# Attention over eight heads: turns of one key tile, with weighing on halves of the rows, in place of double steps

## The reference

```python
def _L0_conv_ref(x, Wq, Wk, Wv, Wsc, gamma):
    q = jnp.einsum('bchw,oc->bohw', x, Wq).reshape(b, HEADS, dq, n)
    k = jnp.einsum('bchw,oc->bohw', x, Wk).reshape(b, HEADS, dq, n)
    v = jnp.einsum('bchw,oc->bohw', x, Wv).reshape(b, HEADS, dv, n)
    attn = jax.nn.softmax(jnp.einsum('bhdn,bhdm->bhnm', q, k), axis=-1)
    out = jnp.einsum('bhnm,bhdm->bnhd', attn, v)
    out = out.reshape(b, w, h, HEADS * dv).transpose(0, 3, 1, 2)
    sc = jnp.einsum('bchw,oc->bohw', x, Wsc)
    return gamma * out + sc

x = x + _L0_conv_ref(_gn(x), Wq, Wk, Wv, Wsc, gamma)
```

## Time and profile before

| | |
|---|---|
| median of 3 runs | 3122.99 us (3122.82 to 3123.27) |
| profiled execution: span | 3120.7 us, 119616 instructions |
| busy: TensorE / weight loads | 3078.5 us (99%) / 2183.3 us (70%) |
| busy: VectorE / ScalarE / POOL | 2284.6 (73%) / 2244.3 (72%) / 2787.6 us (89%) |
| DMA | 110.78 MB, 35 GB/s in the mean |

### The profile page before, as it was taken

How to read it: one execution, slowest core, us unless ns; L and a number is a source line. 1 busy time by engine, 2 the same in 40 slices (tenths; PEclk the granted TensorE clock), 3 DMA queues, 4 the chain that set the end, 5 groups by cost and what they waited for, 6 DMA issues and landing times.

```text
span 3120.7 us, 119616 instructions
## 1 busy us (share of the span) xinstructions
PE 3078.5 (99%) x52307; PEld 2183.3 (70%) x52307; DVE 2284.6 (73%) x3624; ACT 2244.3 (72%) x4020; POOL 2787.6 (89%) x2039
## 2 busy tenths in 40 slices
PE   6999999999999999999999999999999999999998
PEld 4677777767777677777777777777776777767766
DVE  7777777777787777777777777777777777777774
ACT  5676787777676777777667677778776767667676
POOL 1788999999898899999889899999988989889899
PEclk9999999999999999999999999999999999999999
DMA  3111110110112011110112111111101010101011
GB/s 130 31 40 39 30 47 23 45 34 23 36 40 59 20 38 41 27 53 25 24 33 57 40 29 41 38 31 46 23 25 24 22 27 20 29 20 28 21 29 30
DMA packets 168968, 110.78 MB, mean 35 GB/s; under 512 B 120320, under 2 KB 166400, under 8 KB 168448
## 3 DMA queue, kind: packets, MB, share of 16 engines
q1 hardware_dynamic: 168448, 103.13, 12.6%
HBM read 56.10 MB, written 18.87 MB: 24 GB/s over the span
## 4 chain that ended last, share of the span: by engine, by line
PE 91%; POOL 5%; ACT 0%; issue 0%; DVE 0%; ACTq 0%; DVEq 0%
PE SL L441 25%; PE PJ L380 19%; PE MX L413 11%; PE OB L465 10%; PE OB L462 9%; PE OB L464 9%; PE PJ L377 6%; POOL PLO L954 5%; PE SL L436 1%; ACT PE L558 0%; POOL half L950 0%; ACT L676 0%; DVE mx L753 0%; DVE PLO L923 0%; PE SL L389 0%
## 5 line engine op out<-in xcount | busy, mean ns | idle before, releaser
L954 POOL TENSOR_TENSOR PLO<-PE 128x768 f16<-128x768 f32 x1727 | 2551.0, 1500 | 266.8 <-ACT PE L558 255.5
L558 ACT ACTIVATE PE<-SL 128x768 f32<-128x768 f32 x1728 | 1307.3, 809 | 27.6 <-PE SL L441 27.5
L462 PE MATMUL OB<-V,PE 128*128 128x65 f16 x10368 | 1048.5, 193 | 6.8 <-POOL PLO L954 5.7
L464 PE MATMUL OB<-V,PE 128*128 128x64 f16 x10368 | 1048.5, 193 | 0.0
L465 PE MATMUL OB<-V,PLO 128*128 128x65 f16 x10368 | 1048.2, 196 | 0.0
L462 PEld LDWEIGHTS OB<-V,PE 128*128 128x128 bf16 x10368 | 965.1, 99 | 58.2 <-POOL PLO L954 11.7
L441 PE MATMUL SL<-QK 64*128 64x384 f16 x10368 | 1000.8, 323 | 0.1
L464 PEld LDWEIGHTS OB<-V,PE 128*128 128x128 bf16 x10368 | 962.5, 97 | 42.9
L566 ACT ACTIVATE MXC<-MX 128x384 f32<-128x384 f32 x864 | 423.3, 490 | 752.2 <-PE MX L413 752.2
L465 PEld LDWEIGHTS OB<-V,PLO 128*128 128x128 f16 x10368 | 963.4, 98 | 0.0
L753 DVE TENSOR_REDUCE mx<-MX 128x2 f32<-128x768 f32 x864 | 828.4, 959 | 84.4 <-PE MX L413 38.0
(11 more groups left out here) (105 smaller groups left out, 1237.9 us busy)
## 6 DMA issues: line engine op xcount, KB each, us to landing
gx<-x SPq DMA_DIRECT2D x36, 768.0 KB, 4.7
xr<-x SPq DMA_DIRECT2D x96, 192.0 KB, 2.4
out<-xr SPq DMA_DIRECT2D x96, 192.0 KB, 1.9
X<-x SPq DMA_DIRECT2D x6, 768.0 KB, 8.5
CR<-c SPq DMA_TRANSPOSE x96, 2.4
back<-half SPq DMA_TRANSPOSE x95, 2.8
QK<-wk SPq DMA_DIRECT2D x1, 1024.0 KB, 12.7
QK<-wv SPq DMA_DIRECT2D x1, 1024.0 KB, 13.4
```

The lines of the kernel that those rows point to most:

```text
L462: pe.matmul(acc, upper, v[:, D:V1], start=k == 0 and h == 0 and i == 0, stop=False, skip_group_check=True)
L464: pe.matmul(acc[:, 0:D], upper, v[:, 0:D], start=False, stop=False, skip_group_check=True)
L558: act.activation(PE32[:, s % PB, :].rearrange("p (h n) -> p h n", h=2), SL[s % 2][:, :, 0:CH], ACT.Exp, scale=1.0 / SS).then_inc(s_exp, 1)
L954: nc.gpsimd.tensor_tensor(PLO[:, s % PB, :], PE32[:, s % PB, :], PE32[:, s % PB, :].bitcast(BF16)[:, 1:4 * CH:2], ALU.subtract).then_inc(s ...
```

## The change

The loops run over 18 turns of one key tile. TensorE's turn is: scores of the step, one half of the weighing of the step three before (`LAG`), maxima, the other half of the weighing, and in the turns 0, 2, 4 and so on to 14 six terms of a unit (`SLOTS`), a unit in two such turns. Weighing uses halves of the rows: each product is done as two of 64 rows, one with head 0's columns on one half and one with head 1's on the other, to different banks; in its second part the halves have changed heads, and it waits for the first part's end (`s_half`). `SL` has one buffer of two banks, so the scores wait for the exponential just before; `OB` and `PJ` have two banks each. The maxima of both heads are reduced by one operation in each turn, without a copy. The key's upper 16-bit part is copied from `KF` instead of PSUM. The other engines' work is spread over turns anew.

```diff
+LAG = 3
...
+STARTS = (0, 4, 8, 12)
+SLOTS = (6, 0, 6, 0) * 4 + (0, 0)
+TERMS = 3 * CT
+def block_of(k):
+    b = max(i for i, at in enumerate(STARTS) if at <= k)
+    lo = sum(SLOTS[STARTS[b]:k])
+    return b, lo, lo + SLOTS[k]
...
+def done_at(s):
+    if s < 0:
         return None
+    n, k = divmod(s, MT)
+    if k - 2 not in STARTS:
+        return None
+    return unit_in(4 * n + block_of(k)[0])
...
-        SLS = ctx.enter_context(nc.psum_tensor("SL", [P, 4, 512], F32))
-        SL = [SLS[:, 2 * i:2 * i + 2, :] for i in range(2)]
+        SL = ctx.enter_context(nc.psum_tensor("SL", [P, 2, 512], F32))
         MX = ctx.enter_context(nc.psum_tensor("MX", [P, 2, 512], F32))
-        OB = ctx.enter_context(nc.psum_tensor("OB", [P, 512], F32))
-        PJ = ctx.enter_context(nc.psum_tensor("PJ", [P, 512], F32))
+        OB = ctx.enter_context(nc.psum_tensor("OB", [P, 2, 512], F32))
+        PJ = ctx.enter_context(nc.psum_tensor("PJ", [P, 2, 512], F32))
...
             def score(n, k):
-                if s >= 2:
-                    pe.wait_ge(s_exp, s - 1)
+                if s:
+                    pe.wait_ge(s_exp, s)
...
+            def weigh(s, part):
...
+                if part == 0:
...
+                        pe.wait_ge(s_rest, s + 1)
...
+                    pe.wait_ge(s_half, s + 1)
+                cross = (s + part) % 2
+                for i in range(QT):
+                    for piece in range(3):
+                        for half_rows in range(2):
+                            r = slice(half_rows * D, (half_rows + 1) * D)
+                            h = half_rows ^ cross
+                            p0 = h * CH + i * P
+                            acc = OB[:, h, i * OW:i * OW + AW]
+                            v = V[r, g % 2, k, h * V1:(h + 1) * V1]
...
+                last.then_inc(s_half if part == 0 else s_av, 1)
...
             for n in range(CHUNKS):
+                for k in range(MT):
+                    s = n * MT + k
                     U = s + LEAD
+                    b, lo, hi = block_of(k)
+                    score(n, k)
+                    if s >= LAG:
+                        weigh(s - LAG, 0)
                     if U < TOPS:
                         top(U)
+                    if s >= LAG:
+                        weigh(s - LAG, 1)
+                    for i in range(lo, hi):
+                        slot(4 * n + b, i)
...
         def _(act):
+                for k in range(MT):
+                    s = n * MT + k
+                    if k == LAG and n:
                         evacuate(n - 1)
                     exps(s)
+                    if done_at(s):
+                        leave(done_at(s))
+                    if done_at(s - 1) and done_at(s - 1)[0] == "k":
+                        keys_upper(done_at(s - 1))
+                    if done_at(s - 2) and done_at(s - 2)[0] == "k":
+                        keys_diff_upper(done_at(s - 2))
+                    if n and k in (4, 5, 7):
+                        divide(n - 1, (4, 5, 7).index(k))
+                    if n and k == 8:
+                        result_upper(n - 1)
...
         def _(dve):
+                for k in range(MT):
+                    if k == LAG and n:
+                        invert(n - 1)
                     if U < TOPS:
                         top(U)
+                    if done_at(s):
+                        leave(done_at(s))
+                    if stats_part(n, k):
...
+                    if k == 14 and n + 1 < CHUNKS:
                         shift_parts(n + 1)
+                    if k in (6, 10) and n >= 2:
+                        add_result(n - 2, (6, 10).index(k))
...
         def _(pool):
+                for k in range(MT):
+                    if n and k == 9:
                         result_lower(n - 1)
+                    done = done_at(s - 3)
                     if done and done[0] == "k":
                         keys_diff_lower(done)
...
+                    if s + 1 < STEPS:
+                        split(s)
```

More of the change, by code:

```diff
@@ L98, in units @@
     out = [(kind, 0, c) for kind, c in FIRST + BESIDE]
-    for n in range(CHUNKS):
-        out += [done_at(n * DS + m) for m in range(DS) if done_at(n * DS + m)]
+    out += [unit_in(J) for J in range(4 * CHUNKS) if unit_in(J)]
     out.append(("f", CHUNKS - 1))
@@ L106 @@
 PLACE = {u: i for i, u in enumerate(UNITS)}
[L107 to L111, removed]
+LEFT = {u: i + 1 for i, u in enumerate(u for u in UNITS if u[0] != "k")}
 UPPER = {u: i + 1 for i, u in enumerate(u for u in UNITS if u[0] in "qv")}
@@ L262, in norm_piece, with norm_part @@
             return (g % PAIRS - 1) * (NCH // 2) + c - NCH // 2
-        def norm_part(n, m, late):
+        def norm_part(n, k, turns):
             g, c = divmod(n, NCH)
-            if norm_piece(n) is None or not 0 <= m - late < CT:
+            if norm_piece(n) is None or k not in turns:
                 return None
-            return (g // PAIRS, norm_piece(n), m - late)
+            return (g // PAIRS, norm_piece(n), turns.index(k))
         @block.sync
@@ L382, in project, with term @@
                 if hi == 6:
                     last.then_inc(s_pj, 1)
-            def root(b, part):
+            def term(u, i):
+                kind, dst = u[0], bank(u)
+                g, c = divmod(u[1], NCH) if kind == "sc" else u[1:]
+                b, j = divmod(g, PAIRS)
+                t, (wp, p) = i // 3, PARTS3[i % 3]
+                edge = dict(stop=i == TERMS - 1, skip_group_check=True)
+                if kind == "v":
+                    for a in range(QT):
+                        m = c * QT + a
+                        last = pe.matmul(dst[:, a * P:(a + 1) * P], X[:, b % 2, p, t, m * P:(m + 1) * P],
+                                         WT[:, 2, wp, t, j * P:(j + 1) * P], start=i == 0 and a == 0, **edge)
+                    return last
+                return pe.matmul(dst[:, 0:CH], WT[:, WEIGHT[kind], wp, t, j * P:(j + 1) * P],
+                                 X[:, b % 2, p, t, c * CH:(c + 1) * CH], start=i == 0, **edge)
@@ new lines, in slot, with root @@
+            def slot(J, i):
+                u = unit_in(J)
+                if not u:
+                    return
+                if i == 0:
+                    left(same_bank_before(u))
+                    if u[0] == "k" and u[1] % PAIRS == 0:
+                        pe.wait_ge(s_gno, NCH * (u[1] // PAIRS))
+                last = term(u, i)
+                if i == TERMS - 1:
+                    last.then_inc(s_pj, 1)
+            def root(b, part, U):
+                pe.wait_ge(s_gv, 3 * b + 1 + part)
@@ L396, in turn @@
                 for i in range(QT):
[L397 removed]
+                    last = pe.transpose(bank(u)[:, i * P:(i + 1) * P], attn[:, i * P:(i + 1) * P], identf[:, :])
                 last.then_inc(s_pj, 1)
@@ new lines, in weigh @@
+                for i in range(QT):
[6 more added lines that the diff above has]
+                            v = V[r, g % 2, k, h * V1:(h + 1) * V1]
+                            begin = k == 0 and part == 0 and i == 0 and piece == 0
+                            end = k == MT - 1 and part == 1 and i == QT - 1 and piece == 2
+                            upper = PE32[r, s % PB, p0:p0 + P].bitcast(BF16)[:, 1:2 * P:2]
+                            if piece == 0:
+                                last = pe.matmul(acc, upper, v[:, D:V1], start=begin, stop=False,
+                                                 skip_group_check=True)
+                            elif piece == 1:
+                                last = pe.matmul(acc[:, 0:D], upper, v[:, 0:D], start=False, stop=False,
+                                                 skip_group_check=True)
+                            else:
+                                last = pe.matmul(acc, PLO[r, s % PB, p0:p0 + P], v[:, D:V1], start=False,
+                                                 stop=end, skip_group_check=True)
```

314 lines of the change are left out of this document (110 added, 204 removed).

## The result

The changed kernel takes 3564.26 us (median of 4 runs, 3563.39 to 3564.86), the kernel before 3123.05 in the same session: a ratio of 1.1412, with a 95% interval of 1.1396 to 1.1429. The forecast was 3559.

The account below looks back on a forecast made before the run. TensorE's own order was taken as the bound for 90 chunks, POOL in the last block. Opening 86.9, 90 x 36.4 = 3276, +9, -2.4, 149 and 38.1 gave 3556.6 us of span, plus 2.3 around it: 3559 us; range 3440 to 3860.

Parts of the forecast that it names:

- The single score buffer: Scores wait for the exponential just issued: a 1.55 us loop against 1.26 us of TensorE's work in turns without products.
- Turns with products: TensorE's turns with six products and two changes: 2.43 us each, eight a chunk, hiding the score buffer's loop.
- The wait inside the weighing: Weighing's second part waits for the end of its first: between 0 and 0.1 us a turn, taken at 0.05.
- Pairs of half-row products: Weighing's 36 half-row products, issued in pairs to different banks: 31 ns a pair, low end 28, high end 62.
- The rival with 50 to 62 ns: Short weighing pairs do not run side by side: 3791 us at 50 ns, 4092 at 62; chance 0.20.
- Additions: VectorE's result additions in turns 6 and 10 delay the next reduction: 0.6 us stall twice a chunk, +1.2 us.
- Shift rows: Made in turn 14, landing 2.4 us after sending, with turns until 4.65 us: costed at nothing, 0.3 us high end.
- The next image's normalisation: In 18 chunks one statistics operation follows the reduction behind turn 10's addition: 18 x 0.5 = +9 us.
- the last block: Five chunks of 29.8 us each, 149 us, then a last chunk without maxima; POOL bound it before the change.
- Other moved steps: Divisions, evacuation of turn 3 and POOL's differences fall under turns with products or weighing's lag: no cost.
- The signs: TensorE idle some 0.3 us before scores, 0.6 before maxima of turns 8 and 12; POOL's exponential waits near 25%.
- The rival on the faster side: The single score buffer costs nothing and TensorE's order alone counts: 3087 us; chance 0.02.

Follow-up runs that it names:

- e8: Kernel before, with each score step waiting for the exponential of the step just before it, second buffer still there: 4078.6 us, ratio 1.3060.
- e1: Changed kernel with head 1's exponential left out after the first four steps: 3428 us, ratio 1.0974.
- e4: Changed kernel with three projection products in each of 16 turns in place of six in each of 8: 3467.1 us, ratio 1.1101.
- e10: Kernel before, with head 1's exponential left out after the first four steps, as a control: 3135.5 us, ratio 1.0040.
- e2: Changed kernel with the scores moved between the two parts of the weighing: 3523.9 us, ratio 1.1281.
- e3: Changed kernel with the two additions of results in turns 8 and 12 in place of 6 and 10: 3527.5 us, ratio 1.1296.
- e6: Changed kernel with scores between the weighing parts, additions in turns 8 and 12, shift rows made in turn 13 in place of 14: 3455.2 us, ratio 1.1065.
- e7: Kernel of e6 with three projection products in each of 16 turns: 3405.0 us, ratio 1.0906.
- e9: Kernel of e6 with head 1's exponential left out after the first four steps: 3294.9 us, ratio 1.0551.
- e11: Kernel of e9 with head 0's maxima alone reduced from the third chunk on, all products kept: 3157.0 us, ratio 1.0109.

## Why the prediction was right

The measured time is 5 us from the forecast and inside its own range. The mechanism and the sign were right. The terms are less exact than the sum: the additions alone were 67 us too high, smaller errors the other way made up for it, and that is luck.

**The single score buffer** was the large term and the right mechanism. 1.55 us was forecast, 1.57 came (from 1500.07 to 1501.64 above); the first score pair has 0.173 us to the next, not 0.1625, and the rest is rounding. e8 shows the wait by itself, e1 and e4 that the time comes back when the exponential is short or products stand in each turn, e10 that it is the buffer's and not the exponential's.

**Turns with products**: 2.43 forecast, 2.48 measured. The wait inside the weighing was taken at 0.05 and is 0.067; scores take 0.498 from their first start to the weighing in place of 0.487; the rest is in the products' burst. e2 gives the wait back.

**Pairs of half-row products**: 31 ns forecast, 31.2 measured. The rival with 50 to 62 ns fell, and with it, for products in different row halves, the reading of the Trainium skill, "TensorE: Matmul & The Clock Gate", section "Wait — 56ns, not 53.3ns?", by which no two starts are nearer than some 25 ns. The section "The mechanism" of the same page, tiles some 4 ns apart, agrees with this trace: within a pair the starts are 4.1 ns apart in the mean.

**Additions**: +1.2 us a chunk forecast, +0.45 measured (turns 8 and 12, 2.70 and 2.71 against 2.48). This is the term that was mis-sized. The place and the chain were right (e3), but the stall before the maxima is 0.29 us and not 0.6: the addition was taken at 0.8 us and is 0.61 in the middle, and VectorE's three operations were added up by their lengths, while above they start only 0.48 and 0.52 us after each other. Of the 0.29 the turn keeps 0.22, since the inner wait of the weighing, which follows the stalled maxima, runs out during the stall. The row of line 762, after, beside the earlier trace rows:

```profile
L762 DVE SCALAR_TENSOR_TENSOR xr<-back,gam,xr x190: 580/609/1917, 174.2 to 3556.6; 128x384 f32<-128x384 f16 x190
```

**Shift rows**: costed at nothing. Turn 17 is 0.24 us too long in the mean, and two causes share this; its median is 1.57. Over the 84 chunks of the middle 0.17 is the shift rows': their transpose mostly lands 2.3 us after its issue, but in 24 of these chunks it took 3.15 to 4.42, and each cost what it took beyond 3.1. The forecast had that slack right (4.65 - 1.6). What it lacked was the spread: it took 3.3 us, from a short window, for the longest, where the whole trace of the kernel before has 4.6. e6, which sends them a turn earlier, takes off the 0.17 and leaves 0.07. The other 0.07 is the next image's normalisation: in six chunks two small products stand at the end of turn 17, wait for the reduction to free the maxima bank, and cost 0.97 us.

**The next image's normalisation**: 9 us were forecast for 18 statistics operations. These cost next to nothing (turn 12 took 2.73 us with one and 2.70 without). What cost were the six turns 17 just named, 6 us, and three chunks in which ScalarE takes a square root ahead of the exponential of turn 1, with a table load of 1.28 us before it and one behind it:

```profile
379.46 1.28 ACT L697 ACT_TABLE_LOAD   x1
380.75 0.20 ACT L697 ACTIVATE gn<-gn 128x4 f32<-128x4 f32 x1
380.98 1.28 ACT L597 ACT_TABLE_LOAD   x1
...
383.13 0.11 PEld L461 LDWEIGHTS SL<-QK 64*128 64x128 f16 x4 [1.40 <-ACT PE L597]
```

There turn 1 takes 2.73 us instead of 1.57, and turn 12 of the same chunk 3.75 instead of 2.70, with the addition at 1.67 us; together 7 us. Before the change the same two loads were there (344.46 and 346.77) and cost the 0.42 us of waiting in the earlier trace rows, which the forecast read only for a hand-over time.

Together, in a plain chunk, in us: additions -0.75, turns with products 8 x 0.05 = +0.4, turns without 10 x 0.017 = +0.17, shift rows +0.17. That is nearly nothing, which no single term is. Over the 90 chunks 3282.6 us were forecast (3276, +9 and -2.4) and 3283.7 came. In the last block the chunk was 31.1 for 29.8, +6 us for five. The additions there take 1.45 and 1.91 us in turn, but e6, with the three stalls mended, has 31.2 to 31.7 in that block, so they are not the cause, and it stays open; POOL is busy for 137.7 of the 155.3 us. The opening was 1 us shorter, the end 0.5: 3562.5 us of span for 3556.6.

**Other moved steps** were costed at nothing, and no wait for ScalarE's divisions, the evacuation or POOL's splits heads the waits of TensorE in the changed kernel; the table loads above are what lay outside that cover. e7 shows what their cover was: without six products in turn 2 the evacuation costs 0.3 us a chunk.

**The signs.** Scores waited for the exponential 880 times, 0.24 us each (960 times some 0.3 forecast). The idle time before the maxima of turns 8 and 12 came too, half as long as forecast. POOL waited 649.7 us for exponentials, 18% of the span (25% forecast).

**The rival on the faster side** was priced from its point of decision, 1.23 us of return against 0.9 of work, and that is how it fell; e9 and e11 show that it takes two shortened returns, the exponential's and the reduction's, and three mended stalls to come near it.

## What to carry to other kernels

Before a buffer is given up, add up its whole return (last product's end, hand-over, the reader's duration, hand-over) and compare it with the shortest stretch of other work between two uses, turn by turn and not in the mean: here 1.23 us stood against 0.9 in ten turns of eighteen, though every engine had time to spare on the average. Filler work helps only where it stands: spread over the turns it paid for eight more pairs of array changes. When one such loop is shortened, look for the next one with nearly the same period before promising the gain.

## What the runs showed that I had not expected

The addition of results, a VectorE operation whose tensor operands are all in SBUF (float32 and float16 in, float32 out), and POOL's splits do not share time, they take turns. Where no split holds it up the addition takes 0.61 us. In the kernel before, 185 of the 190 additions took more than 0.7 us, and each of these ended 0.41 to 0.42 us after the end of a split; a split that started during an addition took 1.78 us in the median, the others 1.47. The other addition to `xr`, which has one operand in PSUM, kept its length in the same kernel:

```profile
L722 DVE SCALAR_TENSOR_TENSOR xr<-PJ,xr x96: 540/547/560, 97.0 to 3102.3; 128x384 f32<-128x384 f32 x96
```

In the last block of the changed kernel an addition started at 3389.44, POOL's next split at 3389.47; the addition lasted 1.91 us, until 0.41 us after that split's end. It need not have been the first for that: the reduction before it on VectorE (3388.56, 0.96 us long) ended only at 3389.52.

```profile
3388.05 6.05 POOL L959 TENSOR_TENSOR PLO<-PE 128x768 f16<-128x768 f32 x4
...
3389.44 1.91 DVE L762 SCALAR_TENSOR_TENSOR xr<-back,gam,xr 128x384 f32<-128x384 f16 x1
```

And in e10 one addition took 5.65 us. It began in the fourth of seven splits without a gap, and ended 0.41 us after the seventh; another as long made the second slow chunk:

```profile
2984.92 10.01 POOL L955 TENSOR_TENSOR PLO<-PE 128x768 f16<-128x768 f32 x7
...
2989.70 5.65 DVE L742 SCALAR_TENSOR_TENSOR xr<-back,gam,xr 128x384 f32<-128x384 f16 x1
...
2995.87 0.50 PE L413 MATMUL MX<-QK 64*128 64x384 f16 x2 [4.31 <-DVE mx L751]
...
2995.80:2999.00 3.20, 3.13 (x42) 2.40 (x44) 1.43 (x3) 0.00 (x0) 0.00 (x0) 0.55 0.00 0
```

The third row is what it cost: the reduction stood behind the addition, and TensorE stood still for 4.31 us before the next maxima. The last row is a window of the 3.2 us that follow, in the order of the earlier trace rows: the granted clock is 0.55 there, near its lower level (1.2 GHz), so that TensorE loses more time after its wait. The second slow chunk has both as well (4.32 us, and 0.62 from 3056 to 3059). The seven splits ended when POOL had no exponential left, since TensorE made no scores meanwhile.

My taking 0.8 us as something between 0.61 and 1.24, as if POOL slowed the addition in proportion, was therefore the wrong picture: the rest of its time is waiting, and how long that is depends on where POOL stands and whether POOL's next operation is ready. What rule decides between them when both are ready was not tried; in the kernel before 188 of the 190 additions had the end of one split in their time and none had more, in e10 two had four.
